# Three small adapter products of a bank placed one by one between the six large products of the same bank

## The chip, the cores and the metric

One NeuronCore of a Trainium2 chip runs the kernel. The metric is device time in microseconds (us) of one launch, from the first to the last instruction of that core, without the host. TensorE is the engine PE of the profile; its weight loads are listed apart, as PEld. VectorE is DVE, ScalarE is ACT, GpSimd is POOL, SyncE is SP.

## The reference, cut to what matters

`x` is 64 samples x 64 channels x 512. Three layers that add to `x` come first (each sample picks a 64x64 matrix), and then a gated block with low-rank adapters of rank 16, one of 8 adapters per sample:

```python
def _lora_linear(x, W, A, B, adapter_indices):
    base = jnp.einsum('bsd,df->bsf', x, W)
    Ai = A[adapter_indices]
    Bi = B[adapter_indices]
    lora = jnp.einsum('bsr,brf->bsf', jnp.einsum('bsd,bdr->bsr', x, Ai), Bi)
    return base + lora
gate = _lora_linear(x, Wg, Ag, Bg, adapter_indices)   # 512 -> 2048
up = _lora_linear(x, Wu, Au, Bu, adapter_indices)     # 512 -> 2048
h = jax.nn.silu(gate) * up
return _lora_linear(h, Wd, Ad, Bd, adapter_indices)   # 2048 -> 512
```

The change touches the second factor of the adapters of gate and up: the product of `x A` (called `u` in the kernel, made earlier) with `B` (called `b_got`), which is added to `x W` in the same PSUM bank.

## The kernel before

The 64 samples are done in four quarters (`q`), the 2048 hidden columns in 16 blocks of 128 (`b` = 0 to 15). In each of the 64 pairs (q, b), gate and up are made together, for two halves of the tokens, by seven products of a Strassen-Winograd scheme on operands that other engines have summed: A11, S1, S2, A12, S3, S4, A22. Their results are gathered in three PSUM banks, px, py and pz, of 128 partitions x 512 tokens.

**Large products.** Each of the seven is 256 deep (two chunks of 128) and is made with split operands: high part times high part, high times low, low times high. So `product` issues 2 x 3 = 6 matmuls of 128x128 weights (`wg_hi` or `wg_lo`) against 512 moving columns (`xo_hi` or `xo_lo`), at line 1735 by way of `split_product`. They all add into one bank.

**Small products.** `lora` adds the adapters' part to a bank. The samples of the bank are in three chunks, so it issues three matmuls at line 1752, with 128x128 weights from `b_got` and 192, 256 and 192 moving columns from `u`. Each writes only the tokens of its chunk. A block has four such groups of three: (t=0, m=0) on pz behind A12, (t=0, m=1) on py behind S4, (t=1, m=1) on pz, which starts that bank anew and has no large product, and (t=1, m=0) on px behind A22.

**What sets the order.** Every engine has its program written out by hand, with waits on semaphores; there is no scheduler. The code below is TensorE's. In one block it issues A11 into px, S1 into py, S2 into px, A12 into pz with its small group, S3 into px, S4 into py with its small group, the small group of pz alone, A22 into px with its small group, and then one or two phases of the down projection (`down`: 24 large matmuls of 512 columns into the banks pd0 to pd3, at the same line 1735, and 8 of 256 columns into pv at lines 1779 and 1781, in two runs of four).

**Waits around the small groups.** `b_got` holds the rows of B for two blocks (m picks the block's half by `first`, t the half of the tokens). POOL gathers it anew from `b_table` by three indirect DMAs for t=0, once `p3_mm` says that S4's small group of the odd block is done, and three for t=1 after `p4_mm`. `b_got_in[0]` and `b_got_in[1]` count their landings; `u_done` counts the parts of `u`. The last matmul of a bank raises `p2_mm` (A12), `p3_mm` (S4) or `p4_mm` (A22), on which DVE (`c11`, line 1555), ACT and SP wait.

Of the kernel before, what the change touches and what calls it, by code (L numbers as in the profile page):

```python
# [14 lines left out]
P = 128  # L15
# [11 lines left out]
TOK = TP * P  # L27
# [10 lines left out]
A11, S1, A12, S2, A22_T3, S3, A22 = range(7)  # L38
S4 = A22_T3
# [17 lines left out]
CHUNKS = 3  # L57
# [36 lines left out]
def cond_resid_kernel(nc, x, subject, adapter, w0_rows, w1_pairs, w2_rows, bias_pairs, w_gu, w_dn, a_in_rows, ad_rows, b_rows, bd_rows, out):  # L94
# [6 lines left out]
    with ExitStack() as ctx:  # L101
        def sb(name, shape, dt=F32):
            return ctx.enter_context(nc.sbuf_tensor(name, shape, dt))

        def bank(name):
            return ctx.enter_context(nc.psum_tensor(name, [P, 512], F32))

        def sem(name):
            return ctx.enter_context(nc.semaphore(name))

        xo_hi = sb("xo_hi", [P, 7, KH], F32R)
        xo_lo = sb("xo_lo", [P, 7, KH], F32R)
        acc = sb("acc", [P, 2, QP, T])
        u = sb("u", [P, 2, 2, U_COLS], F32R)
        vacc = sb("vacc", [P, 2, TOK])
        w_raw = sb("w_raw", [P, 3, 4, WH])
        wg_hi = sb("wg_hi", [P, 7, WH], F32R)
        wg_lo = sb("wg_lo", [P, 7, WH], F32R)
# [3 lines left out]
        b_got = sb("b_got", [P, 2 * CHUNKS, BW], F32R)  # L122
# [36 lines left out]
        px = bank("px")  # L159
        py = bank("py")  # L160
        pz = bank("pz")
# [159 lines left out]
        p2_mm = sem("p2_mm")  # L321
        p7_mm = sem("p7_mm")
        p3_mm = sem("p3_mm")
        lora22_mm = sem("lora22_mm")
        p4_mm = sem("p4_mm")
# [36 lines left out]
        def unit(q, b):  # L362

            return q * UNITS + b + 1
# [5 lines left out]
        def blocks_done(q, b):  # L370
            return q * BLOCKS + b + 1
# [32 lines left out]
        def chunk(c):  # L404

            n = CHUNK_SAMPLES[c] * C
            return slice(U_FROM[c] * C, U_FROM[c] * C + n), slice(CHUNK_FROM[c] * C, CHUNK_FROM[c] * C + n)
# [27 lines left out]
        def summed_units(n):  # L435

            return n - n // UNITS
# [10 lines left out]
        def weight_slot(n, k):  # L448

            return k ^ 1 if summed_units(n) % 2 and k < A22 else k  # L450
# [29 lines left out]
        def pair_at(q, b):  # L480

            i = b - PAIRS_FROM
            return i if q + 1 < QUARTERS and 0 <= i < QP else None
# [1247 lines left out]
        def _(pe):  # L1731
            def split_product(psum, w_parts, x_parts, start=True, stop=True, more=False):

                for i, (wi, xi) in enumerate(((0, 0), (0, 1), (1, 0))):
                    ins = pe.matmul(psum, w_parts[wi], x_parts[xi], start=(start and i == 0),  # L1735
                                    stop=(stop and i == 2), skip_group_check=more)
                return ins

            def product(psum, k, n, start, stop):

                for c in range(2):
                    ws, xs = slice(c * P, (c + 1) * P), slice(c * TOK, (c + 1) * TOK)
                    ins = split_product(psum[:, :], [w[:, weight_slot(n, k), ws] for w in (wg_hi, wg_lo)],
                                        [s[:, k, xs] for s in (xo_hi, xo_lo)],
                                        start=(start and c == 0), stop=(stop and c == 1), more=not start)
                return ins

            def lora(psum, b, m, t, start=False):
                for c in range(CHUNKS):
                    first = (b % 2) * 2 * P + m * P  # L1750
                    cols, tokens = chunk(c)
                    ins = pe.matmul(psum[:, tokens], b_got[:, CHUNKS * t + c, first:first + P], u[:, m, t, cols],  # L1752
                                    start=(start and c == 0), stop=True, skip_group_check=not start or c > 0)
                return ins

            def warm_up(count, psum=px):
# [9 lines left out]
            def tokens_ready(q, k):  # L1766
                if q:
                    pe.wait_ge(xop_in[k], q * 2 * 16)
                elif k in (A11, A12):
                    pe.wait_ge(o_a1_done, 1)  # L1770
                else:
                    pe.wait_ge(o_done, LOW_ORDER.index(k) + 1)
# [139 lines left out]
            for j in range(TP):  # L1912
                ins = pe.matmul(pv[:, j * C:(j + 1) * C], w1_four[:, j, :], e2_four[:, j, :], start=True, stop=True)
# [75 lines left out]
            for q, b in units():  # L1989
                n = unit(q, b)  # L1990
                i = pair_at(q, b)
# [3 lines left out]
                k = blocks_done(q, b)  # L1995
# [53 lines left out]
                    pe.wait_ge(u_done, 6 * q + 2)  # L2049
                if fresh:  # L2050
                    tokens_ready(q, A12)
                product(pz, A12, n, True, True)

                def lora11():
                    pe.wait_ge(b_got_in[0], (q * SUPER + b // 2 + 1) * CHUNKS * 16)
                    pe.wait_ge(u_done, 6 * q + 3)
                    lora(pz, b, 0, 0).then_inc(p2_mm, 1)

                if n > 1:
                    lora11()  # L2060

                pe.wait_ge(w_done[2], n + 1)
                pe.wait_ge(s2_kept, k)
# [2 lines left out]
                product(px, S3, n, False, True).then_inc(p7_mm, 1)  # L2066
                if n == 1:

                    lora11()
                if i is not None:  # L2070
                    if i < 2:
                        pe.wait_ge(x_in[(q + 1) % 2][i], ((q + 1) // 2 + 1) * 16)
# [2 lines left out]
                              start=True, stop=True).then_inc(layer_mm, 1)  # L2075
# [7 lines left out]
                pe.wait_ge(s5_kept, k)  # L2083
                if fresh:
                    tokens_ready(q, S4)
                product(py, S4, n, False, True)
                lora(py, b, 1, 0).then_inc(p3_mm, 1)

                def lora22():
                    pe.wait_ge(c11_done, k)  # L2090
                    pe.wait_ge(b_got_in[1], (q * SUPER + b // 2 + 1) * CHUNKS * 16)
                    pe.wait_ge(u_done, 6 * q + 6)
                    lora(pz, b, 1, 1, start=True).then_inc(lora22_mm, 1)
# [5 lines left out]
                pe.wait_ge(u3_done, k)  # L2099
                if fresh:  # L2100
                    tokens_ready(q, A22)
                product(px, A22, n, False, True)
                if b == 0:
                    pe.wait_ge(b_got_in[1], (q * SUPER + 1) * CHUNKS * 16)
                    pe.wait_ge(u_done, 6 * q + 6)
                lora(px, b, 0, 1).then_inc(p4_mm, 1)
                if b == 0:

                    lora22()
# [94 lines left out]
```

## Time and profile before

| | us |
|---|---|
| median of 3 runs | 1239.54 |
| lowest and highest | 1239.38 and 1240.88 |
| the profiled execution's own time | 1237.63 |
| its span, first to last instruction | 1235.8 |
| PE busy | 1227.7 (99%), 6190 matmuls |
| PEld busy | 1029.7 (83%), 6190 loads |
| DVE, ACT, POOL busy | 957.1, 558.1, 710.7 |

The granted TensorE clock is the full 2.4 GHz in all 40 slices of the page but for rounding (every digit is 9, the mean is 1.00). A matmul is pipelined: its row lasts from its start to its modelled end, which lies behind the start of the next one. So the row's length (389 ns for 512 columns) is no price; the distance from one start to the next is. This distance is called a slot below.

### The profile page before, as it was taken

Reading aid. Unit: us, or ns where it says so; the run is one execution under the profiler, and the core shown is the slowest. Engines: PE = TensorE matmul, PEld = TensorE weight load, DVE = VectorE, ACT = ScalarE, POOL = GpSimd, SP = SyncE. Lnnn points to the kernel's source line nnn. Section 1 sums busy time; section 2 is a strip of 40 time slices with the busy share of each in tenths; the row PEclk is TensorE's granted clock in tenths of the full one; section 3 lists DMA queues with packets and bytes.
Section 4 is the critical chain, followed back from the end, with each engine's and each line's share of the span. In section 5 each row is a group of like instructions: output and inputs, shape, how many; then the busy total and the mean of one; then the engine's idle time right before and its main releaser. Section 6 shows DMA issues by size and latency. Waiting matters only on the chain.

```text
span 1235.8 us, 18085 instructions
## 1 busy us (share of the span) xinstructions
PE 1227.7 (99%) x6190; PEld 1029.7 (83%) x6190; DVE 957.1 (77%) x1540; ACT 558.1 (45%) x1003; POOL 710.7 (58%) x598
## 2 busy tenths in 40 slices
PE   9999999999999999999999999999999999999998
PEld 8888888888888888888888888888888888888886
DVE  7887777887688777788678778777868877677775
ACT  4744445444544344454344444444534443444333
POOL 4676655558736556546864556555675554444453
PEclk9999999999999999999999999999999999999999
DMA  6866455556865455557496544546659442322323
GB/s 213 295 214 220 126 153 186 162 163 185 289 223 162 124 158 144 164 162 213 142 332 191 178 128 143 166 137 187 198 180 314 160 120 80 93 84 86 113 89 107
DMA packets 141690, 209.60 MB, mean 170 GB/s; under 512 B 44192, under 2 KB 88480, under 8 KB 141600
## 3 DMA queue, kind: packets, MB, share of 16 engines
q1 hardware_dynamic: 117696, 135.45, 34.8%
q0 software_dynamic: 23040, 71.85, 19.0%
q8 instruction: 51, 0.84, 0.3%
q10 hardware_dynamic: 864, 1.15, 0.3%
q14 instruction: 39, 0.32, 0.1%
HBM read 164.36 MB, written 44.04 MB: 169 GB/s over the span
## 4 chain that ended last, share of the span: by engine, by line
PE 97%; DVE 2%; issue 0%; ACT 0%; POOL 0%; DVEq 0%; POOLq 0%
PE px L1735 29%; PE pd L1735 28%; PE py L1735 14%; PE pz L1735 7%; PE pz L1752 3%; PE pv L1781 2%; PE pv L1779 2%; PE pd L2074 2%; PE py L1752 2%; PE px L1752 2%; PE pd L1762 1%; PE px L1886 1%; PE py L1886 1%; PE pd L1871 1%; PE px L1758 1%; PE pd L1904 0%
## 5 line engine op out<-in xcount | busy, mean ns | idle before, releaser
L803 POOL TENSOR_TENSOR h_lo<-g,h_hi 128x512 fp32r<-128x512 f32 x127 | 182.4, 1437 | 298.0 <-ACT h_hi L943 297.2
L766 POOL DMA_INDIRECT b_got<-b_table,idx_b x192 | 198.5, 1034 | 59.9 <-issue 49.9
L1735 PE MATMUL px<-xo_hi,wg_hi 128*128 128x512 f32 x516 | 207.2, 402 | 1.3 <-DVE wg_lo L1382 0.9
L1513 DVE TENSOR_TENSOR acc<-pd,acc 128x512 f32<-128x512 f32 x248 | 164.3, 684 | 51.6 <-PE pd L1735 51.6
L1382 DVE TENSOR_TENSOR wg_lo<-w_raw,wg_hi 128x512 fp32r<-128x512 f32 (+1 forms) x256 | 182.8, 720 | 26.5 <-ACT wg_hi L943 26.4
L1735 PE MATMUL px<-xo_hi,wg_lo 128*128 128x512 f32 x516 | 202.5, 392 | 0.0
L1735 PE MATMUL px<-xo_lo,wg_hi 128*128 128x512 f32 x516 | 201.0, 389 | 0.0
L943 ACT ACTIVATE wg_hi<-w_raw 128x512 fp32r<-128x512 f32 (+1 forms) x260 | 146.0, 570 | 121.1 <-PE py L1752 74.6
L1735 PE MATMUL pd<-wd_hi,h_hi 128*128 128x512 f32 x504 | 199.7, 396 | 0.0
L1735 PE MATMUL pd<-wd_lo,h_hi 128*128 128x512 f32 x504 | 197.9, 393 | 0.0
L1735 PE MATMUL pd<-wd_hi,h_lo 128*128 128x512 f32 x504 | 196.6, 390 | 0.0
L943 ACT ACTIVATE h_hi<-g 128x512 fp32r<-128x512 f32 x128 | 80.9, 632 | 195.0 <-DVE g L1607 76.1
L1735 PEld LDWEIGHTS px<-xo_hi,wg_lo 128*128 128x128 f32 x516 | 96.8, 188 | 22.1
L1735 PEld LDWEIGHTS px<-xo_hi,wg_hi 128*128 128x128 f32 x516 | 96.9, 188 | 19.1 <-issue 2.3
L1735 PEld LDWEIGHTS pd<-wd_hi,h_lo 128*128 128x128 f32 x504 | 94.6, 188 | 21.8
L1735 PE MATMUL py<-xo_hi,wg_hi 128*128 128x512 f32 x260 | 111.6, 429 | 0.0
L1735 PEld LDWEIGHTS px<-xo_lo,wg_hi 128*128 128x128 f32 x516 | 97.5, 189 | 15.6
L1735 PEld LDWEIGHTS pd<-wd_hi,h_hi 128*128 128x128 f32 x504 | 94.6, 188 | 13.9
L1735 PEld LDWEIGHTS pd<-wd_lo,h_hi 128*128 128x128 f32 x504 | 94.8, 188 | 12.8
L1617 DVE TENSOR_TENSOR g<-g,up 128x512 f32<-128x512 f32 x64 | 100.4, 1569 | 3.6 <-ACT g L1181 2.7
L943 ACT ACTIVATE g<-px 128x512 f32<-128x512 f32 x64 | 38.2, 598 | 141.2 <-PE px L1735 141.2
L1735 PE MATMUL py<-xo_hi,wg_lo 128*128 128x512 f32 x260 | 101.8, 391 | 0.0
(331 smaller groups left out, 2439.6 us busy)
## 6 DMA issues: line engine op xcount, KB each, us to landing
w_raw<-w_gu SPq DMA_DIRECT2D x65, 512.0 KB, 4.8
wd_raw<-w_dn SPq DMA_DIRECT2D x64, 256.0 KB, 3.5
xo_hi<-xops SPq DMA_DIRECT2D x21, 512.0 KB, 6.0
xo_lo<-xops SPq DMA_DIRECT2D x21, 512.0 KB, 7.3
acc<-x SPq DMA_DIRECT2D x8, 1024.0 KB, 6.8
ad_raw<-ad_table SPq DMA_DIRECT2D x16, 512.0 KB, 4.3
ad_table<-ad_rows_kept SPq DMA_DIRECT2D x12, 512.0 KB, 6.5
xops<-st_hi SPq DMA_DIRECT2D x24, 256.0 KB, 2.8
```

Source lines behind the costliest of these rows:

```text
L766: gp.indirect_dma_start(out=dst, out_offset=None, in_=rows_of, in_offset=bass.IndirectOffsetOnAxis(ap=rows.bitcast(U32), axis=0)).then_inc ...
L803: return gp.tensor_tensor(dst, src_raw, src_hi, ALU.subtract)
L943: return act.activation(dst, src, ACT.Copy)
L1382: dve.tensor_tensor(wg_lo[:, lo:hi, :], weights_of(n, g), wg_hi[:, lo:hi, :], ALU.subtract).then_inc(w_done[g], 1)
L1513: ins = dve.tensor_tensor(dst, pd[j][:, :], dst, ALU.add)
L1617: dve.tensor_tensor(g1[:, :], g1[:, :], up1[:, :], ALU.mult).then_inc(h_done[1], 1)
L1735: ins = pe.matmul(psum, w_parts[wi], x_parts[xi], start=(start and i == 0), stop=(stop and i == 2), skip_group_check=more)
L1752: ins = pe.matmul(psum[:, tokens], b_got[:, CHUNKS * t + c, first:first + P], u[:, m, t, cols], start=(start and c == 0), stop=True, skip_ ...
L1779: pe.matmul(pv[:, tok], ad[:, half, 2 * t + a, :, :].rearrange("p g n -> p (g n)"), hs[0][:, tok], start=(half == 0 and a == 0), stop=True ...
L1781: ins = pe.matmul(pv[0:HC, tok], ad[:, half, 2 * t + a, 0, :], hs[1][:, tok], start=False, stop=True, skip_group_check=True)
L1886: ins = pe.matmul(ua_bank(q, t, 0)[:, a * HALF:(a + 1) * HALF], w_parts[wi][:, cols], (xo_hi, xo_lo)[xi][:, k, tok], start=(cp == c == a = ...
L2074: pe.matmul(pd[0][:, :], f_one[:, :], acc[:, (q + 1) % 2, PAIR_ORDER[i], :], start=True, stop=True).then_inc(layer_mm, 1)
```

## The change

The three small matmuls of a bank go behind the second, the fourth and the sixth of its large matmuls, where they all stood behind the sixth. This is done for three of the four groups of a block. Groups of the first block of a quarter (b = 0) stay as they were on pz and px; on py they are changed there too. The group that starts its bank (pz, t=1, m=1) stays. No matmul is added or taken away. For A12 the waits for `b_got_in[0]` and `u_done` now stand ahead of the first large matmul.

```diff
+            def lora_chunk(psum, b, m, t, c, start):
+                first = (b % 2) * 2 * P + m * P
+                cols, tokens = chunk(c)
+                return pe.matmul(psum[:, tokens], b_got[:, CHUNKS * t + c, first:first + P], u[:, m, t, cols],
+                                 start=start, stop=True, skip_group_check=not start)
...
+            def product_and_lora(psum, k, n, start, b, m, t):
+
+                for c in range(2):
+                    ws, xs = slice(c * P, (c + 1) * P), slice(c * TOK, (c + 1) * TOK)
+                    w_parts = [w[:, weight_slot(n, k), ws] for w in (wg_hi, wg_lo)]
+                    x_parts = [s[:, k, xs] for s in (xo_hi, xo_lo)]
+                    for i, (wi, xi) in enumerate(((0, 0), (0, 1), (1, 0))):
+                        ins = pe.matmul(psum[:, :], w_parts[wi], x_parts[xi], start=(start and c == i == 0),
+                                        stop=(c == 1 and i == 2), skip_group_check=not start)
+                        if (3 * c + i) % 2:
+                            ins = lora_chunk(psum, b, m, t, (3 * c + i) // 2, False)
                 return ins
...
-                product(pz, A12, n, True, True)
-
-                def lora11():
+                def lora11_ready():
                     pe.wait_ge(b_got_in[0], (q * SUPER + b // 2 + 1) * CHUNKS * 16)
                     pe.wait_ge(u_done, 6 * q + 3)
-                    lora(pz, b, 0, 0).then_inc(p2_mm, 1)
-
-                if n > 1:
-                    lora11()
+
+                if b:
+                    lora11_ready()
+                    product_and_lora(pz, A12, n, True, b, 0, 0).then_inc(p2_mm, 1)
+                else:
+                    product(pz, A12, n, True, True)
+                    if q:
+                        lora11_ready()
+                        lora(pz, b, 0, 0).then_inc(p2_mm, 1)
...
-                product(py, S4, n, False, True)
-                lora(py, b, 1, 0).then_inc(p3_mm, 1)
+                product_and_lora(py, S4, n, False, b, 1, 0).then_inc(p3_mm, 1)
...
-                product(px, A22, n, False, True)
                 if b == 0:
+                    product(px, A22, n, False, True)
                     pe.wait_ge(b_got_in[1], (q * SUPER + 1) * CHUNKS * 16)
                     pe.wait_ge(u_done, 6 * q + 6)
-                lora(px, b, 0, 1).then_inc(p4_mm, 1)
+                    lora(px, b, 0, 1).then_inc(p4_mm, 1)
+                else:
+                    product_and_lora(px, A22, n, False, b, 0, 1).then_inc(p4_mm, 1)
```

On TensorE, A12 and the start of S3 of a block with b > 0, before (a row is one matmul with its load, out<-moving,weights and moving shape, and the semaphores that it waits for):

```order
L1735 MATMUL pz<-xo_hi,wg_hi 128x512 [waits c22_done]
L1735 MATMUL pz<-xo_lo,wg_hi 128x512
L1735 MATMUL pz<-xo_hi,wg_lo 128x512
L1735 MATMUL pz<-xo_hi,wg_hi 128x512
L1735 MATMUL pz<-xo_lo,wg_hi 128x512
L1735 MATMUL pz<-xo_hi,wg_lo 128x512
L1752 MATMUL pz<-u,b_got 128x192 [waits u_done,b_got_in0]
L1752 MATMUL pz<-u,b_got 128x256
L1752 MATMUL pz<-u,b_got 128x192
L1735 MATMUL px<-xo_hi,wg_hi 128x512 [waits s2_kept,w_done2]
```

And the same place on TensorE after the change:

```order
L1766 MATMUL pz<-xo_hi,wg_hi 128x512 [waits u_done,b_got_in0,c22_done]
L1766 MATMUL pz<-xo_lo,wg_hi 128x512
L1751 MATMUL pz<-u,b_got 128x192
L1766 MATMUL pz<-xo_hi,wg_lo 128x512
L1766 MATMUL pz<-xo_hi,wg_hi 128x512
L1751 MATMUL pz<-u,b_got 128x256
L1766 MATMUL pz<-xo_lo,wg_hi 128x512
L1766 MATMUL pz<-xo_hi,wg_lo 128x512
L1751 MATMUL pz<-u,b_got 128x192
L1735 MATMUL px<-xo_hi,wg_hi 128x512 [waits s2_kept,w_done2]
```

The last matmul of the bank is a small one in both, and the bank's place in the order is the same; two small ones have moved forward, and the wait for `b_got_in[0]` and `u_done` by six large matmuls.

On TensorE, the small groups of py and pz behind S4, of the same block, before:

```order
L1735 MATMUL py<-xo_hi,wg_lo 128x512
L1752 MATMUL py<-u,b_got 128x192
L1752 MATMUL py<-u,b_got 128x256
L1752 MATMUL py<-u,b_got 128x192
L1752 MATMUL pz<-u,b_got 128x192 [waits u_done,b_got_in1,c11_done]
L1752 MATMUL pz<-u,b_got 128x256
L1752 MATMUL pz<-u,b_got 128x192
L1735 MATMUL px<-xo_hi,wg_hi 128x512 [waits u3_done,w_done3]
```

And after:

```order
L1766 MATMUL py<-xo_hi,wg_hi 128x512
L1751 MATMUL py<-u,b_got 128x256
L1766 MATMUL py<-xo_lo,wg_hi 128x512
L1766 MATMUL py<-xo_hi,wg_lo 128x512
L1751 MATMUL py<-u,b_got 128x192
L1751 MATMUL pz<-u,b_got 128x192 [waits u_done,b_got_in1,c11_done]
L1751 MATMUL pz<-u,b_got 128x256
L1751 MATMUL pz<-u,b_got 128x192
L1766 MATMUL px<-xo_hi,wg_hi 128x512 [waits u3_done,w_done3]
```

Of six small matmuls in a row, four are left in a row.

## Rows read from the trace of the kernel before

**Rows 1.** The page: TensorE's busy time, and the chain that ended last, by engine.

```profile
PE 1227.7 (99%) x6190; PEld 1029.7 (83%) x6190; DVE 957.1 (77%) x1540; ACT 558.1 (45%) x1003; POOL 710.7 (58%) x598
...
PE 97%; DVE 2%; issue 0%; ACT 0%; POOL 0%; DVEq 0%; POOLq 0%
```

**Rows 2.** Waits of PE, all: who waited for whom, total us, times, longest.

```profile
PE px L1758 <- POOL ident L810: 1.9, 1, 1.9
PE px L1735 <- DVE wg_lo L1382: 0.9, 1, 0.9
PE px L1735 <- DVE up L1560: 0.4, 1, 0.4
```

**Rows 3.** The small products' line: count, ns min/median/max, first and last start, forms.

```profile
L1752 PE MATMUL pz<-u,b_got x384: 249/264/305, 48.0 to 1214.2; 128*128 128x192 f32 x128, 128*128 128x256 f32 x64
...
L1752 PE MATMUL py<-u,b_got x192: 249/254/305, 51.3 to 1213.9; 128*128 128x192 f32 x128, 128*128 128x256 f32 x64
```

**Rows 4.** Weight loads in order of time around pz's small group: start us, length us.

```profile
300.10 0.19 PEld L1752 LDWEIGHTS pz<-u,b_got 128*128 128x128 f32 x1
...
300.21 0.19 PEld L1752 LDWEIGHTS pz<-u,b_got 128*128 128x128 f32 x1
300.33 0.19 PEld L1735 LDWEIGHTS px<-xo_hi,wg_hi 128*128 128x128 f32 x1
300.44 0.19 PEld L1735 LDWEIGHTS px<-xo_lo,wg_hi 128*128 128x128 f32 x1
300.67 0.19 PEld L1735 LDWEIGHTS px<-xo_hi,wg_lo 128*128 128x128 f32 x1
```

**Rows 5.** The chain in order of time: start us, us that it advances, what.

```profile
298.90 1.36 PE pz L1735 x6
300.26 0.32 PE pz L1752 x3
300.58 1.41 PE px L1735 x6
301.99 1.38 PE py L1735 x6
303.37 0.32 PE py L1752 x3
303.69 0.34 PE pz L1752 x3
304.03 1.41 PE px L1735 x6
305.43 0.32 PE px L1752 x3
```

**Rows 6.** Two stretches of 12 large matmuls: window, us, PE busy (count), clock, DMA, GB/s.

```profile
300.42:303.20 2.78, 2.78 (x14) 1.00 0.16 47
313.43:316.15 2.72, 2.72 (x13) 1.00 0.54 170
```

**Rows 7.** Matmuls in order of time around a run of four with 256 columns.

```profile
307.00 0.28 PE L1779 MATMUL pv<-h_hi,ad 128*128 128x256 f32 x1
...
307.46 0.40 PE L1735 MATMUL pd<-wd_hi,h_hi 128*128 128x512 f32 x1
307.70 0.40 PE L1735 MATMUL pd<-wd_lo,h_hi 128*128 128x512 f32 x1
307.93 0.39 PE L1735 MATMUL pd<-wd_hi,h_lo 128*128 128x512 f32 x1
```

**Rows 8.** A gather of b_got, its time to landing, and the products that need it.

```profile
258.17 0.95 POOL L766 DMA_INDIRECT b_got<-b_table,idx_b  x1 [0.30 <-issue]
...
DMA to landing us min/median/max: 3.3/4.3/4.9
...
263.81 0.39 PE L1735 MATMUL pz<-xo_hi,wg_hi 128*128 128x512 f32 x1
...
265.17 0.48 PE L1752 MATMUL pz<-u,b_got 128*128 128x192 f32 x3
```

More of the change, by code:

```diff
@@ L1746, in product @@
                 return ins
+            def lora_chunk(psum, b, m, t, c, start):
[3 more added lines that the diff above has]
+                                 start=start, stop=True, skip_group_check=not start)
             def lora(psum, b, m, t, start=False):
                 for c in range(CHUNKS):
[L1750 to L1753, printed above, removed]
+                    ins = lora_chunk(psum, b, m, t, c, start and c == 0)
+                return ins
+            def product_and_lora(psum, k, n, start, b, m, t):
[8 more added lines that the diff above has]
+                            ins = lora_chunk(psum, b, m, t, (3 * c + i) // 2, False)
                 return ins
@@ L2067, in _ @@
                 if n == 1:
-                    lora11()
+                    lora11_ready()
+                    lora(pz, b, 0, 0).then_inc(p2_mm, 1)
                 if i is not None:
```

## The prediction

> **What bounds the kernel now.** I read the page first: TensorE is busy 99% of the span of 1235.8 us, and the chain that ended last is TensorE for 97% [rows 1]. Then its waits: three in all, 3.2 us together [rows 2]. So nothing that another engine does holds TensorE back, and the time is the sum of the slots (start to start) of 6190 matmuls. A change in their order is worth what it does to slots, and nothing else.
>
> What sets a slot is seen in the order of time. A weight load starts where the matmul before it starts, never sooner. In a run of large matmuls that is every 0.227 us (12 of them in 2.72 us [rows 6]), and a load of 0.11 us of port time is hidden in that. Among the small ones the starts of the loads are 300.10, 300.21, 300.33, 300.44, and then 300.67 [rows 4]. So the slots in the chain of loads are 0.11 (192 columns), 0.12 (256) and 0.11 (192), and the large one behind them has its 0.23 again. The reader is to see that the third step, 300.33 to 300.44, is the load of the **large** one's successor waiting for the large one's own load: a slot of 0.11 belongs to each small matmul with 192 columns, whatever stands behind it.
>
> How much of it is stall? 512 columns take 0.227 us [rows 6] and 256 take 0.115 us (four from 307.00 to 307.46 [rows 7]), so a column is worth (0.227 - 0.115) / 256 = 0.44 ns, and 192 columns would stream in 0.115 - 64 x 0.00044 = 0.087 us. The slot is 0.11. So 0.02 us is a stall on the next load, in each matmul with 192 columns; one with 256 has next to none.
>
> **The change part by part.** It adds and removes no matmul, no load and no transfer. It moves two of three small ones forward in 60 groups on pz, 64 on py and 60 on px: 184 groups of the 256 (the first block of each of the four quarters keeps pz and px; the fourth group stays). [rows 3] show the forms: two of 192 columns and one of 256 in each group.
>
> *The stall of the small ones.* A load for a small matmul between large ones is hidden, but so was the first load of each group before. The load for what comes behind a small matmul must fit under that matmul, whether the next one is small or large. Before, three loads per group stand under a small matmul (second, third, next large); after, again three (three large). So 3 x 0.11 stays 3 x 0.11: zero. The nearest rows say that a row of small ones costs the same per matmul however long it is: three advance the chain by 0.32 and six by 0.32 + 0.34 = 0.66 us, each followed by 1.41 us for the six large [rows 5]. With the late load of about 0.02 in that 1.41 (load at 300.44 for a matmul that started at 300.42), three cost 0.34 and six 0.68. A fixed price of one such row, F, is 2 x 0.34 - 0.68 = 0.00, with 0.01 of rounding. The change makes 2 more rows of small ones per group, 368 in all. Taken: F = 1 ns, 0.4 us in sum, since the two rows lie next to zero; bounds 0 and 10 ns, 0 and 3.7 us.
>
> *The pace of large ones behind small ones.* Six large ones take 1.36 us when many large ones stand ahead (first of [rows 5]), 1.41 right behind small ones, and 1.38 as the second six. Of the 0.05, 0.02 is the late load that is counted above; 0.03 over six, 5 ns each, is a slower pace, which lasts some ten large matmuls: twelve take 2.78 behind small ones and 2.72 settled [rows 6]. I can't say from the trace what makes it. Behind a run with 256 columns it is there too: 307.46 to 307.70 to 307.93 is 0.24 and 0.23 [rows 7].
> After the change, large ones that ran settled stand behind a small one. A12 is all settled before (1.36): four of its six are then behind a small one, 4 x 5 = 20 ns, x 60 = 1.2 us. S4 is half settled (1.38): its last four lose some 2.5 ns each, 10 ns x 64 = 0.6 us. A22, S3 and the first of the down phase stand behind small ones already (1.41): nothing. Sum 1.8 us. Bounds: if one small matmul unsettles nothing, the 0.02 of S4 and the 0.03 of A22 are given back, and A12 loses nothing: -0.05 x 62 = -3.1 us. If each large one behind a small takes 0.24 as the first in rows 7 (13 ns over settled), A12 and S4 lose 4 x 13 ns in 124 groups, and A22 half of it in 60: 8.0 us.
>
> *The wait that moved.* For A12 the wait for `b_got_in[0]` is now 1.36 us earlier (263.81 and not 265.17 [rows 8]). Behind it on TensorE stands everything, so any lateness is paid in full. It can bind only where the rows were just gathered, in the 28 even blocks behind the first of a quarter. There the third gather is issued at 258.17, lands 4.9 us later at most, at 263.07, and 263.81 is the need: 0.74 us of cover, in a block where there is little. Taken: 0. Nobody else's wait moves: the banks are finished by the same last small matmul, so `p2_mm`, `p3_mm` and `p4_mm` come where they came, some 20 ns later.
>
> *The sum.* 0.4 + 1.8 + 0 = +2.2 us. On the profiled execution's own time of 1237.63 that is 1239.8; on the median of 1239.54, **1241.7 us**, 0.18% more.
>
> *A rule against the trace.* All loads in rows 4 start with the matmul ahead of them, even where the port had been free for 0.1 us; nothing was loaded two matmuls ahead. The Trainium skill, in "TensorE: Matmul & The Clock Gate", section "Architectural detail: the array is 16x 32x32, not 1x 128x128", says that PE's queue is a partial reorder window that can pull weight loads ahead of matmuls in flight. If that held for more than one matmul ahead, this change would be a gain, which is rival D.
>
> **The rivals.** A is the forecast: no stall goes, a little pace is lost.
> B, *slower*: each row of small ones has a fixed price on TensorE that three and six in a row hide in rounding. For: the bounds above allow 10 ns. Against: 0.34 and 0.68. At 10 ns it gives 3.7 + 1.8 = 5.5, so 1245.0. With the pace term of 1.8, it passes 0.2% (2.5 us) from F = 0.7 / 368 = 2 ns on.
> C, *faster by pace*: a single small one leaves the large ones settled, and the recovery that follows a row of three is shorter too. For: the pace depends on what stands ahead, and a row of four with 256 columns is followed by only 0.24, 0.23. Against: every short row in the trace, of any length, is followed by slower large ones. It gives -3.1 us by the bound above, and twice that if S3 and the first six of the down phase (0.03 each) settle as well: -3.1 - 0.06 x 62 = -6.8. Middle: 1234.6.
> D, *faster by loads*: with the queue of large ones ahead, the load behind a small one is done early, and its 0.02 us of stall goes. 368 matmuls with 192 columns x (0.11 - 0.087) = 8.5 us, so 1231.0. Against: rows 4, where no load did that.
> E, *a late gather*: if the last gather lands over 0.7 us later than in this trace, A12 waits in 28 blocks; 0.5 us beyond the cover in each is 14 us, 1253.5. Rows 8 speak against it.
>
> **How the numbers follow.** A 0.66, B 0.15, C 0.12, D 0.04, E 0.03. A's own spread is 1240.2 to 1243.0 (F from 0 to 3 ns, the pace from half to one and a half). A measurement of this kernel tells 0.2%, 2.5 us, from no change: 1237.1 to 1242.0 is the same. A lies there in 0.45 of its 0.66 and above in 0.21; B and E are slower; C and D faster. Faster 0.16, same 0.45, slower 0.39. The range reaches from the near part of C to B: 1236.5 to 1245.0. It leaves out D, E, most of C and the far end of B, about 0.2.
>
> **What would show it.** Right: rows of the chain with each small matmul in 0.11, A12 and its three in some 1.70 us where it took 1.68, S4's nine in 1.71 where they took 1.70, A22's in 1.73 as before; still no wait of PE at line 1766. The loads around a single small one are 0.11 apart, then 0.23. Wrong: a load that starts before the matmul ahead of it (D); large ones at 0.227 two behind a small one (C); a small one of over 0.12 in the chain (B); a wait of PE for DMA b_got (E).

## The result, and the profile after

| | us |
|---|---|
| changed kernel, median of 20 runs | 1241.58 (1240.23 to 1243.92) |
| kernel before, median of 20 runs beside it | 1239.70 (1238.59 to 1241.51) |
| ratio, 95% interval | 1.0017, 1.0010 to 1.0024 |
| span of the profiled execution | 1238.4, before 1235.8 |

The change costs 1.9 us (1.2 to 3.0 by the interval). The forecast was +2.2 us and 1241.7, inside 0.2%. But the sum came out nearly right while the terms of its largest step, the pace of the large matmuls, did not, and the experiments below show that.

The page of the changed kernel, TensorE's busy time and the chain by engine, to be put beside [rows 1]:

```profile
PE 1229.6 (99%) x6190; PEld 1028.5 (83%) x6190; DVE 956.0 (77%) x1540; ACT 559.3 (45%) x1003; POOL 711.3 (57%) x598
...
PE 98%; DVE 1%; DMA 0%; issue 0%; ACT 0%; DVEq 0%
```

TensorE still sets nearly all of the time. Its two longest waits (who waited for whom, total us, times, longest) are those of [rows 2]. Of its three short ones, 1.0 us together, the last matters below:

```profile
PE px L1774 <- POOL ident L810: 1.9, 1, 1.9
PE px L1735 <- DVE wg_lo L1382: 0.8, 1, 0.8
PE pd L1920 <- issue: 0.2, 1, 0.2
```

Line 1766 doesn't stand in this list, so the wait for `b_got_in[0]` that was moved forward is covered. (In the same kernel's second profile it waits once, 0.5 us on px for DVE's `up`. That is the third wait of [rows 2] under its new line.)

Weight loads in order of time around the first two single small matmuls of a group on pz, after the change, to be put beside [rows 4] (start us, length us):

```profile
300.19 0.19 PEld L1766 LDWEIGHTS pz<-xo_hi,wg_lo 128*128 128x128 f32 x1
300.30 0.19 PEld L1766 LDWEIGHTS pz<-xo_hi,wg_hi 128*128 128x128 f32 x1
...
300.76 0.19 PEld L1766 LDWEIGHTS pz<-xo_lo,wg_hi 128*128 128x128 f32 x1
300.87 0.19 PEld L1766 LDWEIGHTS pz<-xo_hi,wg_lo 128*128 128x128 f32 x1
```

The reader is to see 300.19 to 300.30: the small matmul's successor is now a large one, and its load still needs its 0.11 us before the next load starts. The stall has changed its neighbour and not its size. For the one with 256 columns it is 300.76 to 300.87.

These are starts of loads. The starts of the matmuls of the same place are 0.09 apart for the small one of 192 columns (300.19 to 300.27, unrounded 86 ns) and 0.26 for the large one behind it (254 ns), so the stall of some 0.02 us is paid by the matmul that comes next and not by the small one. The pair takes 0.34 us, 0.11 more than a settled large one. Matmuls in order of time:

```profile
300.27 0.42 PE L1766 MATMUL pz<-xo_hi,wg_lo 128*128 128x512 f32 x1
300.53 0.39 PE L1766 MATMUL pz<-xo_hi,wg_hi 128*128 128x512 f32 x1
300.75 0.28 PE L1751 MATMUL pz<-u,b_got 128*128 128x256 f32 x1
```

The second large one behind the small one has 0.22 (227 ns): it runs at the settled pace at once. Behind the one with 256 columns the two large ones have 233 and 236 ns.

The chain in order of time through the products of one block, after, to be put beside [rows 5] (start us, us that it advances, what):

```profile
299.90 0.45 PE pz L1766 x2
300.35 0.09 PE pz L1751
300.44 0.48 PE pz L1766 x2
300.92 0.12 PE pz L1751
301.03 0.47 PE pz L1766 x2
301.50 0.09 PE pz L1751
301.58 1.39 PE px L1735 x6
302.98 0.45 PE py L1766 x2
...
304.67 0.35 PE pz L1751 x3
305.01 0.48 PE px L1766 x2
...
306.75 1.41 PE pd L1735 x6
```

A12 with its three takes 299.90 to 301.58, 1.68 us, as before to 0.01. S3's six large ones behind it take 1.39 and not 1.41. S4 with its three takes 302.98 to 304.67, 1.69 and not 1.70. A22 with its three takes 305.01 to 306.75, 1.74 and not 1.73 (1.41 and 0.32). Nothing here is 20 ns worse at a single place. One piece that the change doesn't touch is longer too: the twelve large matmuls of the down phase between its two runs of four with 256 columns, before

```profile
307.63 2.74 PE pd L1735 x12
```

and after

```profile
308.62 2.76 PE pd L1735 x12
```

The loss is best seen over many blocks. A block's time is nearly the same to the nanosecond each time, so I take two stretches of the trace: **plain** blocks, the twelve from 978.70 to 1187.66 of the kernel before, and **layer** blocks, eight (b = 3 to 10 of the third quarter) which have the layer's product of line 2074 on pd between S3 and S4, and that of line 2041 between S2 and A12 (three of the eight have eight matmuls of line 1762 between S1 and S2 as well). The starts of A11's first matmul at the ends of the plain stretch, before:

```profile
978.70 0.40 PE L1735 MATMUL px<-xo_hi,wg_hi 128*128 128x512 f32 x1
...
1187.66 0.40 PE L1735 MATMUL px<-xo_hi,wg_hi 128*128 128x512 f32 x1
```

and after:

```profile
981.12 0.40 PE L1735 MATMUL px<-xo_hi,wg_hi 128*128 128x512 f32 x1
...
1190.24 0.40 PE L1735 MATMUL px<-xo_hi,wg_hi 128*128 128x512 f32 x1
```

That is 208.96 and 209.12 us, 13 ns in each of twelve blocks. The same reading in the eight layer blocks gives 150.90 and 151.27 us, 47 ns in each.

The third figure that I use below is the **stretch**: from the first matmul of A12 in block b = 1 to the first of the last eight products on lines 1779 and 1781. Before:

```profile
58.94 0.39 PE L1735 MATMUL pz<-xo_hi,wg_hi 128*128 128x512 f32 x1
...
1222.46 0.28 PE L1779 MATMUL pv<-h_hi,ad 128*128 128x256 f32 x1
```

After:

```profile
59.53 0.39 PE L1766 MATMUL pz<-xo_hi,wg_hi 128*128 128x512 f32 x1
...
1225.09 0.28 PE L1795 MATMUL pv<-h_hi,ad 128*128 128x256 f32 x1
```

1163.52 and 1165.56 us: +2.0 us, beside the measured 1.9. But 0.35 of it is no slot. The wait at line 1920 (0.2 us above) stands inside the stretch, and with what follows it, seven matmuls on pd, px and pz take 0.35 us more than before. The same changed kernel, profiled once more, has no wait there, and a stretch of 1165.27 us, +1.75. So what the change does to slots is +1.7 to +1.75 us in the two profiles, and the rest of the +2.0 is a wait that comes in some executions. It comes in four of the fourteen profiles of this text, each time once, and for a DMA where the profile names what ended it.

The stretch leaves out what comes ahead of 59 us, where executions of one kernel differ by more than the change is worth. The second profile came to the first of these matmuls at 62.89 us and not at 59.53. In it TensorE waited 1.46 us for DVE at line 1959. Its matmuls of that line had run for 0.6 us when its clock fell to the lower of its two levels, 1.2 GHz, from 20.3 to 23.7 us. The rows are the matmuls with their wait (start us, us, what), and a stretch of the low clock (window, us, PE busy (count), clock, DMA share, GB/s):

```profile
19.70 5.37 PE L1959 MATMUL pd<-acc 128*128 128x512 f32 x8 [1.46 <-DVE acc L1387]
20.00:22.00 2.00, 2.00 (x4) 0.56 0.31 73
```

### The profile page after: what moved, and what is told of

Read it like the earlier page. It is cut to its first block, busy times and chain, and to the rows that moved or that the text cites. A ratio compares the mean times of both kernels' runs of the same rounds, so it can differ in the third digit from the quotient of the medians.

```text
span 1238.4 us, 18085 instructions
## 1 busy us (share of the span) xinstructions
PE 1229.6 (99%) x6190; PEld 1028.5 (83%) x6190; DVE 956.0 (77%) x1540; ACT 559.3 (45%) x1003; POOL 711.3 (57%) x598
## 4 chain that ended last, share of the span: by engine, by line
PE 98%; DVE 1%; DMA 0%; issue 0%; ACT 0%; DVEq 0%
PE pd L1735 28%; PE px L1735 22%; PE py L1766 7%; PE py L1735 7%; PE px L1766 7%; PE pz L1766 7%; PE pz L1751 3%; PE pv L1797 2%; PE pv L1795 2%; PE pd L2094 2%; PE px L1751 2%; PE py L1751 2%; PE pd L1778 1%; PE py L1902 1%; PE px L1902 1%; PE pz L1735 1%
## 5 line engine op out<-in xcount | busy, mean ns | idle before, releaser
L1735 PE MATMUL px<-xo_hi,wg_hi 128*128 128x512 f32 x396 | 158.2, 399 | 0.8 <-DVE wg_lo L1382 0.8
L1735 PE MATMUL px<-xo_lo,wg_hi 128*128 128x512 f32 x396 | 154.7, 391 | 0.0
L1735 PE MATMUL px<-xo_hi,wg_lo 128*128 128x512 f32 x396 | 154.7, 391 | 0.0
L803 POOL TENSOR_TENSOR ad<-ad_raw,ad 128x512 fp32r<-128x512 f32 x32 | 50.6, 1580 | 79.8 <-DVE g L1555 79.2
L1555 DVE TENSOR_TENSOR g<-pz,g 128x512 f32<-128x512 f32 x64 | 44.1, 688 | 62.4 <-PE pz L1751 50.2
L803 POOL TENSOR_TENSOR wd_lo<-wd_raw,wd_hi 128x512 fp32r<-128x512 f32 x64 | 85.2, 1339 | 9.8 <-ACT wd_hi L943 9.7
L1735 PEld LDWEIGHTS px<-xo_hi,wg_hi 128*128 128x128 f32 x396 | 74.3, 188 | 19.1 <-issue 1.7
L1565 DVE TENSOR_TENSOR up<-py,up 128x512 f32<-128x512 f32 x64 | 44.2, 690 | 58.8 <-PE py L1751 56.1
```

The source lines that it names most:

```text
L803: return gp.tensor_tensor(dst, src_raw, src_hi, ALU.subtract)
L1555: dve.tensor_tensor(g0[:, :], pz[:, :], g0[:, :], ALU.add).then_inc(c11_done, 1)
L1565: dve.tensor_tensor(up0[:, :], py[:, :], up0[:, :], ALU.add).then_inc(c12_done, 1)
```

## The experiments

### The three places apart

Four kernels on one chip. All differ from the kernel before only in which groups are split. For the two places that a kernel leaves alone, the edit puts the code of before back:

```diff
-                product_and_lora(py, S4, n, False, b, 1, 0).then_inc(p3_mm, 1)
+                product(py, S4, n, False, True)
+                lora(py, b, 1, 0).then_inc(p3_mm, 1)
...
-                    product_and_lora(px, A22, n, False, b, 0, 1).then_inc(p4_mm, 1)
+                    product(px, A22, n, False, True)
+                    lora(px, b, 0, 1).then_inc(p4_mm, 1)
```

(this is the one that splits pz alone; the other two are made in the same way.) What was expected:

> The change as it is, once more, as a yardstick for the other three. All theories: 1.0017 of the kernel before, +1.5 to +2.7 us.

> Only the 60 groups on pz (A12) are split, with the earlier wait. Theory 1, the steps of the prediction: the pace of A12's settled large matmuls carries most of the loss, +1.2 us and 0.1 for the split, +1.3 us. Theory 2, the place as the trace of the changed kernel has it (A12 longer by 12 ns in 63 blocks, S3 behind it shorter by 17): +0.2 us. Rival 3, one fixed price for each split group: 60 of 184 groups, a third of 2.1 us, +0.7 us. If the moved wait cost anything, this kernel alone would show it, with waits of PE at line 1766.

> Only the 64 groups on py (S4) are split. Theory 1, the steps of the prediction: +0.6 us of pace and 0.1, +0.7 us. Theory 2, by place: S4 8 ns shorter and the group of pz behind it 6 ns longer, 0.0 us, and the rest by what it does to A22 behind it. Rival 3, fixed price: +0.7 us.

> Only the 60 groups on px (A22) are split. Theory 1, the steps of the prediction: A22's large matmuls stand behind small ones already, +0.1 us. Theory 2, by place: A22's bank 15 ns longer in 59 blocks and the down phase behind it 12 ns longer in 64, +1.3 to +1.7 us, nearly the whole loss. Rival 3, fixed price: +0.7 us.

| split | ratio (95%) | stretch, us | per plain block, ns | per layer block, ns |
|---|---|---|---|---|
| all three | 1.0013 (1.0002 to 1.0023) | +1.75 | +13 | +47 |
| pz (A12) | 0.9994 (0.9983 to 1.0004) | -0.2 | -27 | +27 |
| py (S4) | 1.0004 (0.9995 to 1.0014) | +0.9 | 0 | +27 |
| px (A22) | 1.0002 (0.9992 to 1.0011) | +1.2 | +20 | +20 |

The times alone can't tell the three apart; their intervals are 2 us wide. The traces can. The starts of A11 at the ends of the plain stretch, split on pz alone:

```profile
981.35 0.40 PE L1735 MATMUL px<-xo_hi,wg_hi 128*128 128x512 f32 x1
...
1189.99 0.40 PE L1735 MATMUL px<-xo_hi,wg_hi 128*128 128x512 f32 x1
```

208.64 us, 27 ns less per block than before. Split on px alone:

```profile
983.15 0.40 PE L1735 MATMUL px<-xo_hi,wg_hi 128*128 128x512 f32 x1
...
1192.35 0.40 PE L1735 MATMUL px<-xo_hi,wg_hi 128*128 128x512 f32 x1
```

209.20 us, 20 ns more. Where pz gains is in its chain, in order of time:

```profile
303.34 1.39 PE px L1735 x6
304.73 1.36 PE py L1735 x6
306.09 0.32 PE py L1751 x3
```

S4's six take 1.36, the settled pace, where they took 1.38, and S3's take 1.39 and not 1.41. The split on A12 shortens the recovery behind it, in a plain block. Where each of them gains and loses is seen from the sums of the same starts, as a mean over the twelve plain blocks, in ns against the kernel before ("row" is a bank's three small matmuls, wherever they stand):

| split | A12 and row | S3 | S4 and row | row of pz alone | A22 and row | 6 large of down | its first four with 256 | its next 12 large | sum |
|---|---|---|---|---|---|---|---|---|---|
| all three | +11.5 | -17.5 | -9.1 | +6.6 | +14.2 | +1.8 | -6.0 | +11.8 | +13 |
| pz | +11.6 | -17.5 | -20.7 | -0.2 | 0.0 | +0.2 | -0.2 | +0.1 | -27 |
| py | 0.0 | -0.1 | -1.6 | +1.6 | 0.0 | +0.1 | 0.0 | 0.0 | 0 |
| px | -0.2 | +0.1 | +0.1 | -0.1 | +12.4 | +1.8 | -5.8 | +11.7 | +20 |

A11, S1, S2 and the last ten matmuls of a block repeat to 0.2 ns in these kernels, and so they do in those below, though the sets were run on different chips. In a layer block the split on pz gains nothing: A12 is 12 ns longer, S3 3 ns longer and not shorter, S4 with its row 18 ns longer. The product of line 2074 behind S3 can't be why S3 itself gains nothing; A12 is met in another state there, since the product of line 2041 stands right ahead of it. That this is the reason is not shown.

What follows: theory 1, the steps of the prediction, falls for pz (+1.3 expected, -0.2 found) and for px (+0.1 expected, +1.2 found). For py its sum is near (+0.7 and +0.9), and its place is not: it put 10 ns into S4 of every block, and a plain block has 0, a layer block 27, of which S4 has 12 and the rest stands in A22 and in the down phase. Rival 3, one price per split group, falls on pz. Theory 2, by place, is near on pz (+0.2 expected) and px (+1.3 to +1.7), and off on py (0.0 expected). The three stretches add up to +1.9, and all three together have +1.7 to +1.75. That looks additive and is not: in a plain block -27 + 0 + 20 makes -7, and all three have +13; in a layer block 27 + 27 + 20 makes 74, and all three have 47. The two misses cancel.

### What sets the slot of a small matmul

The two outer small matmuls of each of the 256 groups (512 matmuls) get another width, in the order of before and, once, in the split order:

```diff
                 cols, tokens = chunk(c)
+                if c == 0:
+                    cols, tokens = slice(cols.start, cols.start + P), slice(tokens.start, tokens.start + P)
+                if c == 2:
+                    cols, tokens = slice(cols.stop - P, cols.stop), slice(tokens.stop - P, tokens.stop)
```

and for the wide one `2 * P` in place of `P`. These kernels leave out a part of the adapters' product, or add it twice; they are for the time alone.

> The kernel before, with the two small matmuls of 192 columns of each of the 256 groups cut to 128 columns (512 matmuls; the samples at the two outer chunks' inner edges get their part from the middle chunk alone). If the slot of 192 columns is set by the next weight load (the prediction): slots stay 0.11, the time stays within 1 us of the kernel before. If it is set by the columns: 64 x 0.44 ns = 28 ns less in each of 512, -14 us.

> The kernel before, with the small matmuls of 192 columns made 256 wide (512 matmuls, their added columns overlap the middle chunk's, whose part is then added twice there). By the next load (the prediction): the slot goes from 0.11 to 0.115 to 0.12 us, +2 to +5 us. By columns: +28 ns in each of 512, +14 us. If the late load is what unsettles the large ones behind, six of them behind three small ones take 1.36 us where they took 1.41; if any short row unsettles them, 1.39 to 1.40.

> The changed kernel, with the small matmuls of 192 columns cut to 128 in the same way. By the next load: no more than 1 us from the changed kernel, and the large matmul behind each single small one starts its stream later by as much as the small one got shorter (0.06 us and 0.28, where it is 0.09 and 0.25). If a load could be brought forward past a large matmul, the slots would fall to 0.06 and the time by up to 14 us.

| | ratio (95%) | stretch, us | per plain block, ns | per layer block, ns |
|---|---|---|---|---|
| 128 columns, in a row | 1.0004 (0.9993 to 1.0015) | +1.0 | +33 | 0 |
| 256 columns, in a row | 1.0028 (1.0016 to 1.0039) | +4.1, 0.5 of it by the wait at line 1920 | +47 | +80 |
| 128 columns, split | 1.0015 (1.0003 to 1.0026) | +1.9, 0.2 over the changed kernel without its wait | +47 | +21 |

One third fewer columns in each of 512 matmuls bring nothing, in a row and between large ones: by columns it would have been -14 us. One third more cost some 3.6 us, inside the +2 to +5 of the load's theory, and not 14. (The wait at line 1920 is here 1924, by the longer edit.) TensorE's matmuls in order of time, with 128 columns in a row:

```profile
303.42 0.45 PE L1755 MATMUL pz<-u,b_got 128*128 128x128 f32 x3
303.70 0.46 PE L1735 MATMUL px<-xo_hi,wg_hi 128*128 128x512 f32 x1
304.00 0.40 PE L1735 MATMUL px<-xo_lo,wg_hi 128*128 128x512 f32 x1
```

The three start earlier, by 303.70 - 303.42 = 0.28 us where it was 0.32, and the large one behind pays it back: 0.30 us to the next start, where it was 0.25. And split, with 128 columns:

```profile
300.07 0.22 PE L1755 MATMUL pz<-u,b_got 128*128 128x128 f32 x1
300.13 0.45 PE L1770 MATMUL pz<-xo_hi,wg_lo 128*128 128x512 f32 x1
300.41 0.39 PE L1770 MATMUL pz<-xo_hi,wg_hi 128*128 128x512 f32 x1
```

0.06 and 0.28, as expected in numbers: the small one and its successor take 0.34 us together at 128 columns as at 192. So no load comes forward past a large matmul. The starts of the loads say it directly: in none of the fourteen profiles does one of the 6190 loads start before the matmul ahead of its own does; the earliest start 0 or 1 ns behind it, and half of them within 3 ns.

The chain of the kernel with 256 columns throughout tells of the pace:

```profile
301.52 0.35 PE pz L1755 x3
301.88 1.39 PE px L1735 x6
303.26 1.36 PE py L1735 x6
```

No load is late here (each starts within 5 ns of the matmul ahead; with rows of 192 columns some start 20 to 26 ns behind it), and six large ones behind the small ones still take 1.39 and not 1.36. So it doesn't need a late load to unsettle them. The second six are at 1.36, so they recover sooner than behind 192 columns (1.38 [rows 5]). Nor does every short matmul unsettle them: in the changed kernel the first single one with 192 columns, whose load is late, is followed by 254 and then at once by 227 ns, and S3, behind another, has 257 and five times 227. There the single one with 256 columns is what 233 and 236 ns follow.

### The wait that moved

```diff
-                    lora11_ready()
-                    product_and_lora(pz, A12, n, True, b, 0, 0).then_inc(p2_mm, 1)
+                    product_and_lora(pz, A12, n, True, b, 0, 0, lora11_ready).then_inc(p2_mm, 1)
...
+                        if 3 * c + i == 1 and ready is not None:
+                            ready()
                         if (3 * c + i) % 2:
```

> The changed kernel, with the wait for b_got_in[0] and u_done put back from A12's first large matmul to its first small one. If the moved wait costs nothing (the prediction): from the block b = 1 to the end of the last block the same as the changed kernel to 0.3 us. If it costs: less by what it cost.

Ratio 1.0008 (0.9997 to 1.0020); the stretch is 1165.29 us, beside 1165.27 of the changed kernel's second profile and 1165.21 of its first without the 0.35 us at line 1920. Plain and layer blocks have its +13 and +47 ns. The moved wait costs nothing, as forecast.

### The order of widths in a row

If the loss hangs on how large matmuls recover, the order inside a row that is not split should move it too:

```diff
-                for c in range(CHUNKS):
-                    ins = lora_chunk(psum, b, m, t, c, start and c == 0)
+                for c in (0, 2, 1):
+                    ins = lora_chunk(psum, b, m, t, c, start and c == 0)
```

and (1, 0, 2) with `c == 1` for 256 first.

> The kernel before, with the three small matmuls of each of the 256 groups in the order 192, 192, 256 columns. By the next load two of 192 columns stall as before, so nothing is gained in the slots. If what stands directly ahead of the large ones sets how they recover (behind rows of 256 columns alone they are settled after five, behind 192 last after ten): S4 comes back to 1.36 us for its six where it took 1.38, -1.1 us, with up to 0.7 more or less by the down phase. If not: 0.0 us.

> The same with the order 256, 192, 192. Slots as before. By the same reasoning the large ones behind a small one of 192 columns recover as before: within 0.7 us of the kernel before, by the down phase alone.

> Only pz's groups split, as in only_pz (-0.2 us from b = 1 to the last block), and all groups that stay in a row in the order 192, 192, 256. If both effects hold and add up: -1.3 us, the fastest of all. If the pace behind A12 and S3 is settled already, as it is in only_pz, the gain in S4 can't be had twice: -0.2 to -0.5 us.

> pz's groups split (alone -0.2 us from b = 1 to the last block) and the groups that stay in a row in the order 256, 192, 192 (alone -0.7 us). If the effects add up: -0.9 us. They did not with 256 last: +1.3 us where -0.2 and +0.8 make +0.6. If what a short row costs hangs on the state in which it is met, and not on the row: anything between -1.5 and +0.5 us, and the large ones behind the rows in another sequence of slots than in either kernel.

| | ratio (95%) | stretch, us | per plain block, ns | per layer block, ns |
|---|---|---|---|---|
| 256 last | 1.0007 (0.9998 to 1.0016) | +0.9 | +13 | +1 |
| 256 first | 0.9997 (0.9988 to 1.0006) | -0.8 | -27 | 0 |
| pz split, 256 last | 1.0002 (0.9993 to 1.0011) | +1.3, without the wait at line 1920 +0.6 | -7 | +34 |
| pz split, 256 first | 1.0005 (0.9996 to 1.0014) | +0.4, without that wait -0.4 | -33 | +34 |

The wait, longest of all in the last kernel (who waited for whom, total us, times, longest):

```profile
PE pd L1920 <- DMA bd_lo<-bd_table,bias: 0.6, 1, 0.6
```

It makes the seven matmuls around it 0.8 us longer there and 0.6 us in the kernel above it. It is not taken for an effect of the edits, since the changed kernel has it in one profile and not in the other.

With 256 last my expectation of -1.1 us failed, though a part of its mechanism was there. The chain in order of time:

```profile
302.38 0.34 PE pz L1751 x3
302.72 1.39 PE px L1735 x6
304.12 1.36 PE py L1735 x6
```

S4's six came back to 1.36 as expected. But each row of three takes 0.34 and not 0.32, which I had put at "as before". Over a plain block the three rows behind large ones are 75 ns longer, and the large ones behind them (S3, S4, A22, six of the down phase) 72 ns shorter, so the two nearly cancel. The rest of the +13 is the down phase: its first four with 256 columns lose 2 ns and its next twelve large ones are 12 ns longer, as in the changed kernel. With 256 first the rows stay at 0.32 and S4's six are at 1.36 too:

```profile
302.20 0.32 PE pz L1751 x3
302.52 1.41 PE px L1735 x6
303.92 1.36 PE py L1735 x6
305.29 0.32 PE py L1751 x3
```

I had expected nothing beyond 0.7 us of it; it is the best stretch of all, -0.8 us. Of the two kernels with pz split, the one with 256 last adds up in its sum once the wait is left out (-0.21 and +0.85 make +0.64, and +0.63 it is), so its +1.3 is no sign that effects don't add. The one with 256 first doesn't: -0.2 and -0.8 make -1.0, and it has -0.4; in a plain block -27 and -27 would make -53 ns, and it has -33. No kernel here is faster than the one before by more than its interval. 256 first is ahead in the trace alone.

## Why the prediction was right, and where not

*Nothing else than slots* (right in the main). TensorE waits 3.2 us in the profile before and 3.7 in the one after, none of it by the wait that moved. Of the stretch's +2.0 us 0.35 is the wait at line 1920, which the same kernel's second profile doesn't have, and +1.7 is slots.

*The stall of the small ones* (right, and shown). 3 x 0.11 stayed 3 x 0.11, by the starts of the loads. The prediction read it as the slot of the small matmul itself, and that reading is wrong: start to start, the three of a row have 86, 141 and 92 ns and the large one behind them 254, so each stall falls on the next matmul. Its sign "each small matmul in 0.11" is therefore not in the chain, which has 0.09, 0.12 and 0.09 for the single ones; the sum is not changed by it. Rival D, a load brought forward, falls by the loads at 300.19 and 300.30 and by the 128 columns that brought nothing. With it the rule cited from the Trainium skill, "TensorE: Matmul & The Clock Gate", section "Architectural detail: the array is 16x 32x32, not 1x 128x128", reaches no further here than one matmul ahead: a load starts beside the matmul before its own, and never sooner.

*The moved wait* (right, and shown) costs 0.

*The pace of large ones* (the failed step). The size, +1.8 us, was about right (+1.7 found), and its places were wrong. The step said that A12 loses 1.2 us since its settled matmuls come to stand behind a small one, and that S3, A22 and the down phase lose nothing since they are unsettled already. The runs show -0.2 us for pz and +1.2 for px. A12 with its row did lose, 12 ns where 20 were put; but S3 and S4 behind it gained 38 ns in a plain block, which was left to rival C. A22 lost 12 ns where 0 was put, and the down phase behind it 8 more, in matmuls that the prediction didn't look at. The assumption that failed is that the pace is a fixed 5 ns for each large matmul that stands within ten of a small one. What a short row costs depends on the state in which it is met: on A12, where all is settled, the single small ones shorten the recovery behind them; on A22, which follows six small ones, they lengthen it. The term for py (+0.7 against +0.9) is near in its sum alone. Two signs that were named show it: A12 and S4 with their rows were put at 1.70 and 1.71 us and took 1.68 to 1.69 and 1.69.

*The fixed price F* (neither shown nor refuted as such). Rival B at 10 ns per row would give 20 ns for each split group: it falls as it stands, since in a plain block A12 with S3 is 6 ns shorter for the split on pz, and the split on py costs 0. A price of 1 ns can't be told from the changes of the pace.

*Rival C*, faster by pace, holds in part: its sign, a large matmul at 0.227 two behind a small one, is there behind the single ones with 192 columns on pz and py, and in plain blocks the split on pz gives 27 ns back in each. It doesn't hold on px or in layer blocks. *Rival E* did not happen.

A's own spread was added up a little wide of its terms: F = 0 with half the pace is +0.9 us, 1240.4 and not 1240.2, and F = 3 ns with one and a half times the pace +3.8 us, 1243.3 and not 1243.0. Nothing else hangs on it.

So the forecast of the time was right partly by luck: +1.2 us put on pz in place of px, a term for py that is near in sum alone, and misses that cancel between plain and layer blocks.

What stays open is the rule by which the pace goes. A late load is neither needed for it (256 columns throughout) nor enough (a single one with 192), and DMA does not look like it, as blocks repeat to the nanosecond. I have no run that names the part of the chip behind it.

## What to carry to other kernels

Before small matmuls are spread among large ones, ask what is hidden under the **small** one: it is the load of whatever comes next, and that costs 0.11 us for 128x128 weights whether the next one is small or large. Spreading saves this stall only if loads could run ahead by more than one matmul, which the starts of the loads in a trace show in one look. And where a kernel is bound by TensorE with next to nothing waiting, sum its slots over many equal blocks of one trace: that tells 10 ns per block, where times of whole runs can't tell 1 us. A long stretch needs a look for single waits first: one wait for a DMA was worth up to 0.8 us here, as much as most of the differences.

## What the runs showed of the hardware that I had not expected

The differences per plain block of all these kernels fall on multiples of 6.67 ns: 0, 6.7, 13.3, 20, 26.7, 33.3 and 46.6 ns up or down (each is the difference of a stretch of twelve blocks, divided by twelve). In layer blocks they lie within 1 ns of such multiples, 80.0 with 256 columns throughout. 6.67 ns are 16 periods of the granted 2.4 GHz clock. The settled slot of a large matmul, 2.72 us / 12 = 226.7 ns, is 34 of them. Single starts don't keep to such a grid: behind a row the large ones have 254, 229, 233, 236, 224 and 231 ns, and only the settled ones and the sum over a block fall on it. So an edit in the order moved a block, once it had settled again, by whole steps of 6.67 ns, up or down. That is worked out from the starts alone; no run tests what makes it.

The twelve large matmuls of the down phase between its runs with 256 columns take 2747 ns in a plain block of the kernel before and of those split on pz or py alone, 2730 with 128 columns split, and 2758 in all the other kernels, though no edit touches them. A part of what an edit costs stands that far behind it.

The other thing is how much of a time's spread lies ahead of the work: up to 4 us before the first 63. In the profile shown, 1.46 us of it is the wait for DVE and the rest lies for the most part in the 3.4 us at 1.2 GHz that came right behind it. Such a wait alone isn't followed by the lower clock each time: the profile of pz split alone has 1.6 us of it at the same line, and the full 2.4 GHz throughout.
